# Selective scan laid out as 16 states by 8 channels on the partitions, with q and k projected during the scan

## What is computed

```python
qkv = einsum('bysd,ed->byse', x, w_qkv) + b_qkv          # 16 heads of 16
attn = softmax(einsum('bhqd,bhkd->bhqk', q, k) / sqrt(16))
vals = einsum('bhqk,bhkd->bhqd', attn, v)
h = concatenate([einsum('bse,oe->bso', vals, w_out) + b_out, txt], axis=1)   # 589 tokens
u = layernorm(h)
xp = einsum('bld,kd->blk', u, x_proj_w)                  # 64 + 16 (B) + 16 (C)
delta = softplus(einsum('blr,dr->bld', xp[..., :64], dt_proj_w) + dt_proj_b)
# for each token t, channel d (256) and state n (16):
#   h[d, n] = exp(delta[t, d] * A[d, n]) * h[d, n] + delta[t, d] * B[t, n] * u[t, d]
#   y[t, d] = sum over n of h[d, n] * C[t, n]
h = h + y + u * D_skip
```

## Time and profile before

| | us |
|---|---|
| median of 3 runs | 1422.09 |
| lowest, highest | 1415.88, 1423.06 |
| the profiled execution, its own time | 1426.25 |
| its span in the trace | 1424.1 |

### The profile page before, as it was taken

How to read it: one execution, slowest core, us unless ns; L and a number is a source line. 1 busy time by engine, 2 the same in 40 slices (tenths; PEclk the granted TensorE clock), 3 DMA queues, 4 the chain that set the end, 5 groups by cost and what they waited for, 6 DMA issues and landing times.

```text
span 1424.1 us, 14635 instructions
## 1 busy us (share of the span) xinstructions
PE 1044.0 (73%) x4633; PEld 522.9 (37%) x4634; DVE 790.0 (55%) x1271; ACT 457.2 (32%) x693; POOL 171.8 (12%) x217
## 2 busy tenths in 40 slices
PE   7898988888888988835653499995589955047780
PEld 2323332433234332422243255552366644023340
DVE  4603799768995799739935021223355558512224
ACT  1173356424663356442232111111122143011120
POOL 1000000000000000000002322211000002744451
PEclk9898989989998999967865599998699987568886
DMA  2197113111220113112255111112600000048856
GB/s 86 41 309 243 70 63 119 38 45 41 103 102 1 70 43 120 43 70 104 100 217 233 62 44 38 40 38 81 272 1 0 0 1 10 25 170 319 314 184 218
DMA packets 70254, 145.30 MB, mean 102 GB/s; under 512 B 10716, under 2 KB 54973, under 8 KB 66365
## 3 DMA queue, kind: packets, MB, share of 16 engines
q1 hardware_dynamic: 62720, 136.99, 27.9%
q0 software_dynamic: 7488, 7.70, 1.6%
HBM read 113.70 MB, written 43.75 MB: 111 GB/s over the span
## 4 chain that ended last, share of the span: by engine, by line
PE 33%; DVE 27%; issue 22%; POOL 6%; DMA 6%; ACT 5%; SPq 1%; POOLq 1%; DVEq 0%; ACTq 0%
DVE hst L1363 10%; PE ps L566 5%; DVE hC L1371 5%; PE ps L544 4%; DMA ys_dram<-yo,dest 3%; PE ps L863 3%; DVE mxn L1310 2%; PE ps L953 2%; PE ps L908 2%; PE ps L654 2%; POOL xs_dram L1285 2%; PE ps L676 2%; PE ps L881 1%; PE ps L667 1%; POOL ys_dram L1264 1%
## 5 line engine op out<-in xcount | busy, mean ns | idle before, releaser
L676 PE MATMUL ps<-hC,ident 128*128 128x512 f32 (+1 forms) x384 | 155.0, 544 | 72.7 <-DVE hC L1371 72.7
L1310 DVE TENSOR_REDUCE mxn<-ps 128x2 f32<-128x1024 f32 x128 | 151.3, 1221 | 74.2 <-PE ps L566 73.5
L1363 DVE TENSOR_TENSOR_SCAN hst<-dA,dBu 128x1180 f32<-128x1180 f32 x64 | 166.9, 2608 | 0.5
L1042 ACT ACTIVATE Ph<-ps 128x1024 f32<-128x1024 f32 x128 | 124.1, 1021 | 91.1 <-PE ps L654 91.1
L676 PEld LDWEIGHTS ps<-hC,ident 128*128 128x128 f32 x384 | 71.9, 201 | 184.8 <-DVE hC L1371 116.6
L566 PE MATMUL ps<-Kh,Qh 32*128 32x512 f32 x512 | 110.5, 694 | 16.1 <-DVE mxn L1310 13.8
L953 PE MATMUL ps<-ring,xgT 128*64 128x256 f32 x512 | 80.1, 440 | 27.0 <-DVE yo L1731 26.9
L654 PE MATMUL ps<-Qh,Kh 32*128 32x512 f32 x512 | 90.1, 684 | 4.6 <-ACT Ph L1042 4.6
L1354 DVE TENSOR_TENSOR dBu<-dtu,bc 128x1180 f32<-128x1180 f32 x64 | 87.9, 1378 | 0.0
L1249 POOL COPY xa<-home 128x20 f32<-128x20 f32 x1 | 0.2, 218 | 725.0 <-DMA home<-in_home 725.0
L1371 DVE TENSOR_TENSOR hC<-hst,bc 128x1180 f32<-128x1180 f32 x64 | 86.8, 1362 | 0.0
(11 more groups left out here) (239 smaller groups left out, 1477.2 us busy)
## 6 DMA issues: line engine op xcount, KB each, us to landing
bc<-bc_dram SPq DMA_DIRECT2D x64, 590.0 KB, 3.7
ring<-in_we SPq DMA_DIRECT2D x16, 2048.0 KB, 9.3
W<-in_w SPq DMA_DIRECT2D x14, 1024.0 KB, 18.3
xs_dram<-zeros SPq DMA_DIRECT2D x1, 8224.0 KB, 45.4
xg<-xs_dram SPq DMA_DIRECT2D x16, 514.0 KB, 4.3
yg<-ys_dram SPq DMA_DIRECT2D x12, 640.0 KB, 7.9
ys_dram<-zeros SPq DMA_DIRECT2D x1, 5120.0 KB, 49.6
xs_dram<-zeros SPq DMA_DIRECT2D x1, 4112.0 KB, 18.9
```

Source lines behind the costliest of these rows:

```text
L676: m = nc.tensor.matmul(tail[:, lo:hi], ident[:, :], state[:, lo:hi], start=False, stop=(n == NS - 1), skip_group_check=True)
L1042: nc.scalar.activation(Ph[:, n % 2, 2 * g:2 * g + 2, :], ps[:, 2 * g:2 * g + 2, :], ACT.Exp, scale=float(HD) ** -0.5).then_inc(act_p, 1)
L1310: nc.vector.tensor_reduce(slots32(mxn[:, hg % 2, i, :])[:, 2 * g:2 * g + 2, HD], ps[:, 2 * g:2 * g + 2, :], AX.X, ALU.max, negate=True).th ...
L1363: nc.vector.tensor_tensor_scan(hst[:, k % 2, :, :].rearrange("p c t -> p (c t)"), dA[:, k % 2, :, :].rearrange("p c t -> p (c t)"), dBu[:, ...
```

## The change

**Layout of the scan.** A unit now holds 8 channels with all 16 states on the 128 partitions (partition = 8·state + channel), again two such groups beside each other, so there are again 16 units (`UNITS`) for a sample. B and C are the same for all units of a sample and are spread once (`BC`, two loads). delta and delta·u, which were in SBUF for all units, differ for each unit: they are written to DRAM (`dd_dram`, two stores) and each unit loads them back with two loads of 590 KB, each of 8 rows repeated for 16 states (`spread`), into three slots `dd`. The operands of `decay` and `drive` come from `dd`. `output_gate` works in place on `hst`, which has four buffers, and `hC` is gone.

**Sum over the states.** Two units make a set of 32 channels. `add_set` adds it to y with eight matmuls: two pieces of tokens by four column tiles of 32, with 0/1 matrices `bsum`. One half of the channels is accumulated at a time, so `skip` and `take_y` are split in two.

**Projections.** q and k of sample b + 1 are projected while sample b is in `back` (on even steps, through bank 7), into a second buffer of `Qh` and `Kh`. Only v is projected in `front`, ahead of the first scores. Sample 0 still projects in its own front, through banks 5 and 6. `project_x` and `project_dt` come two groups of scores earlier. `Ph` and `OT` share their place with `xn`, `xb`, `sp` and `xpo`, so ACT starts the exponentials of a back only after `dd_out` and the first `decay`.

```diff
+            def spread(b, j):
+                k = UNITS * b + j
+                c, band, lane = place(j)
                 if k >= SLOTS:
                     q.wait_ge(dve_dBu, k - SLOTS + 1)
-                    q.wait_ge(dve_hC, k - SLOTS + 1)
-                q.dma_start(bc[:, k % SLOTS, :, :].rearrange("p w t -> p (w t)"),
-                            bc_dram[b, 2 * n:2 * n + 2].rearrange("(o w) t -> o (w t)", o=1).to_broadcast([P, 2 * LP])).then_inc(bc_in[k % SLOTS], 16)
+                    q.wait_ge(act_dA, k - SLOTS + 1)
+                for m in range(2):
+                    lo = HR * (lane + m) + DD * band
+                    q.dma_start(dd[:, k % SLOTS, m, :, :].rearrange("p w t -> p (w t)"),
+                                dd_dram[b, c, lo:lo + DD].rearrange("(o d) w t -> o d (w t)", o=1).to_broadcast([NS, DD, 2 * LP])).then_inc(dd_in[k % SLOTS], 16)
...
+                for w in range(2):
+                    q.dma_start(BC[:, w, :], bc_dram[b, w].rearrange("n (o t) -> n o t", o=1).to_broadcast([NS, DD, LP])).then_inc(bc_in, 16)
+                q.wait_ge(dve_delta, b + 1)
+                q.dma_start(dd_dram[b, :, :, 0, :].rearrange("c p t -> p c t"), sp[:, :, :]).then_inc(dd_out, 16)
+                q.wait_ge(dve_dtu, b + 1)
+                q.dma_start(dd_dram[b, :, :, 1, :].rearrange("c p t -> p c t"), xb[:, :, :]).then_inc(dd_out, 16)
+                q.wait_ge(dd_out, 32 * (b + 1))
+                for j in range(UNITS):
+                    spread(b, j)
...
+            def add_set(b, k):
+                c, band, _ = place(2 * k)
+                pe.wait_ge(dve_hC, UNITS * b + 2 * k + 2)
+                for lo, hi in pieces(0, LP):
+                    for lane in range(4):
+                        m = nc.tensor.matmul(tail[HR * lane:HR * (lane + 1), lo:hi], bsum[:, band, :], hst[:, (2 * k + lane // 2) % 4, lane % 2, lo:hi],
+                                             start=False, stop=(band == 3), skip_group_check=True)
                 m.then_inc(pe_y, 1)
...
+            def back(eb, cb, qb):
+                for n in range(NU):
                     if eb is not None:
                         tscores(eb, n)
+                        if qb is not None and n % 2 == 0:
+                            project(qb, n // 4, n // 2 % 2, 7)
                         if n:
                             weighted(eb, n - 1)
-                    if cb is not None and n >= 2:
-                        add_state(cb, n - 2)
+                    if cb is not None and n % 2 and n >= 3:
+                        if n == SETS + 3:
+                            skip(cb, 1)
+                        add_set(cb, (n - 3) // 2)
                 if eb is not None:
                     weighted(eb, NU - 1)
                     turn_heads(eb, range(HG - 1))
+                    turn_heads(eb, [HG - 1])
                 if cb is not None:
-                    add_state(cb, NS - 2)
+                    add_set(cb, SETS - 1)
...
+                softplus(nb)
+                act.wait_ge(dd_out, 32 * (nb + 1))
+                decay(nb, 0)
...
+            def drive(b, j):
+                k = UNITS * b + j
+                if j == 0:
+                    dve.wait_ge(bc_in, 32 * (b + 1))
+                dve.wait_ge(dd_in[k % SLOTS], 32 * (k // SLOTS + 1))
+                if k >= 2:
+                    dve.wait_ge(dve_scan, k - 1)
+                nc.vector.tensor_tensor(dBu[:, k % 2, :, :], dd[:, k % SLOTS, :, 1, :], BC[:, 0:1, :].to_broadcast([P, 2, LP]),
```

More of the change, by code:

```diff
@@ L622, in front @@
                     m.then_inc(pe_bo, 1)
+                else:
+                    project_v(mb, 0, 4)
+                    project_v(mb, 1, 3)
                 for hg in range(HG):
@@ L975, in _ @@
             front(0, None)
-            back(0, None)
+            back(0, None, 1)
             for b in range(NB):
-                nxt = b + 1 if b + 1 < NB else None
+                nxt, then = (k if k < NB else None for k in (b + 1, b + 2))
                 front(nxt, b)
-                back(nxt, b)
+                back(nxt, b, then)
             one_expert()
@@ L1073, in front @@
[L1073 to L1084 removed]
+                    take_v(mb, 0, 4)
+                    take_v(mb, 1, 3)
+                standard_deviations(nb)
@@ L1085, in back @@
+                normalise(nb)
+                take_u(nb)
+                take_x(nb)
+                softplus(nb)
+                act.wait_ge(dd_out, 32 * (nb + 1))
+                decay(nb, 0)
+            def back(eb, cb, qb):
+                for n in range(NU):
                     if eb is not None:
                         exps(eb, n)
+                        if qb is not None and n % 2 == 0:
+                            take_q(qb, n // 4, n // 2 % 2, 7)
                         if n % QT == 0 and n:
@@ L1088, in back @@
                             take_o(eb, n // QT - 1)
-                    if cb is not None and n + 1 < NS:
+                    if cb is not None and n == SETS + 2:
+                        take_y(cb, 0)
+                    if cb is not None and n + 1 < UNITS:
                         decay(cb, n + 1)
```

312 lines of the change are left out of this document (143 added, 169 removed).

## The result

The changed kernel is slower: 1464.32 us, median of 4 runs (1450.34 to 1468.55), beside 1418.99 us (1412.38 to 1423.06) of the kernel before on the same chip. The ratio is 1.031, 95% interval [1.022, 1.039]. I had predicted 1437, with 1415 to 1454: the direction was right, the loss is three times as large. Experiments named with one time and no range ran once each (e2, e5 to e10, e13, e14); the kernel before spread over 1404.6 to 1431.1 us in all its runs, so single runs are read here by the stages of their traces.

The account below looks back on a forecast made before the run. DVE was taken to bound scanning backs, PE and ACT alternating back(0, None), waits for scores the fronts. Terms +15 - 1.5 - 0.9 - 2 x (1.5 + 2.0) + 9.3 + 0 gave +14.9 on 1422.09: 1437 us, range 1415 to 1454.

Parts of the forecast that it names:

- Part 1, the scan units: Scans: still 64 units of 5.10 us with DVE never idle, 0 change, up to 60 if the loads bind.
- four loads of the present form move at 295 to 415 GB/s; these cover it: Scan units: the doubled loads need 237 GB/s, and the rate read from the kernel before was taken to suffice.
- loads bind: Rival in the scans: below 237 GB/s loads bind; at 200 GB/s a unit takes 6.0 us, +58, 1495; chance 0.05.
- DVE's small change of work in a unit: Scan units: the same three DVE operations of the same width, 5.10 us for each unit.
- PE's fall: Scanning backs: PE's busy time falls from 69 us to about 59 of 82 us.
- the `pe_y` wait: Scans: the new wait of `recurrence` on `pe_y` looks four units back, with almost one period of slack.
- The trip through DRAM: From the end of `dtu` to the first scan: store and loads take 14 us, mostly hidden except in sample 3.
- Part 2: back(0, None): projecting q and k there adds 15 us, bounds 8 and 16; a pair of groups grows to about 7.2.
- Part 3, the fronts: Three fronts, first scores to first scan: -6.0 at full clock, +4.5 for half clock, so -1.5 each.
- the clock term: Fronts: PE at half clock for about five of twelve groups ahead of `dtu`; 4.5 us taken, from 0 to 8.
- Parts 4 and 6: Joints: -0.9 ahead of front(1, 0), -2 twice; small things: 0, an extra constant +0.5 against shorter last sums -0.5.
- Part 5: Sample 3: joint gains 2, unhidden way from `dtu` to first scan costs +11.3; together +9.3, from 5 to 13.

Follow-up runs that it names:

- e2: Changed kernel with the repeat in the `dd` loads turned round, eight channels outermost and each row written to 16 partitions in a row: 1686.2 us.
- e5: Changed kernel with one source row for all partitions in the `dd` loads, written as 16 times 8 repeats (two outer dimensions): 1465.6 us.
- e10: Kernel before with its `bc` loads written as 16 times 8 repeats of the same row in place of 128: 1424.7 us, beside 1421.3.
- e13: Changed kernel with `dd` loads from 128 different rows, eight taken and eight left out 16 times (two outer dimensions): 1464.2 us.
- e14: Changed kernel with 16 loads for each unit, each of one row for one lane, repeated for 16 partitions eight apart: 1778.1 us.
- e6: Changed kernel with each `dd` load taken from 128 different rows, none repeated, one outer dimension: 1434.6 us.
- e1: Changed kernel with each `dd` load taken from one row repeated for all 128 partitions, in place of eight rows repeated 16 times: 1439.3 us.
- e15: Changed kernel with one-row `dd` loads (one outer dimension) and q and k of sample 1 projected in front(1, 0): 1428.1 us, ratio to before 1.009.

## Why the prediction was wrong

**Part 1, the scan units: the step that failed first.** I predicted 0 and it was +13.8 us in the scans. The step was "four loads of the present form move at 295 to 415 GB/s; these cover it". The changed loads are not of that form. They have a second outer dimension, and move 229 GB/s where a unit needs 237. The rival "loads bind" named the right threshold, and I gave it 0.05, arguing from rows of the same length. e5, e6 and e13, all with rows of that length, show that the form decided. The price was smaller than the rival's 58 us, since the rate is 3% below the need and not 16%: 1.21 MB at 229 GB/s are 5.28 us, 0.18 too long, and 64 times that is 11.5. DVE's small change of work in a unit, PE's fall and the `pe_y` wait were right: with fast loads all scans are 76.8 to 76.9 us (e1, e15).

**The trip through DRAM: right in its form, and slow by the same cause.** I predicted 14 us from the end of `dtu` to the first scan. With the loads of the form that I had priced it is 13.7 to 13.9 (e1); with the real ones it is 19.1, 17.5, 17.6 and 17.4. That is 16.4 us in all, and with the 13.8 of the scans 30.2; the span of e1 is 27.2 us shorter, its median time 25.0. So the loads account for about the whole distance from 1437 to 1464; that my other errors nearly cancel each other is luck.

**Part 2: right.** +13.8 for +15. A pair of groups went from 5.28 to 84.46 - 77.33 = 7.13 us (I had 7.2):

```profile
77.33 1.37 PE L690 MATMUL ps<-Qh,Kh 32*128 32x512 f32 x8
...
84.46 1.14 PE L690 MATMUL ps<-Qh,Kh 32*128 32x512 f32 x8
```

**Part 3, the fronts: the clock term was too small.** From the prediction's terms, 46.2 less 1.2 for the first scores, I had 45.0 us from first maximum to the end of `dtu` at full clock, and 4.5 for the half clock, so 49.5. Measured were 51.2, 53.6 and 53.2, and 51.1 to 53.9 in all the other fronts with this code, at mean clocks of 0.65 to 0.74. That is 6 to 9 for the clock in place of 4.5, if 45.0 is right, which nothing showed: no front without projections ran at full clock. With fast loads the three fronts cost 67.2, 66.0 and 67.2 us from first maximum to first scan, against 65.1, 65.0 and 65.0 before: +5.3 where I had -4.5. Of the fronts' miss (+17.0 for -4.5) 9.8 is the clock and 11.7 the loads. The pace was as predicted, 3.40 us for a group at half clock, but I had it for five of twelve groups, and mean clocks of 0.67 to 0.73 in these stretches mean half clock for more than half of the time:

```profile
515.50 2.36 DVE L1338 TENSOR_REDUCE mxn<-ps 128x2 f32<-128x1024 f32 x2 [1.24 <-PE ps L598]
518.90 2.36 DVE L1338 TENSOR_REDUCE mxn<-ps 128x2 f32<-128x1024 f32 x2 [1.04 <-PE ps L598]
522.31 2.36 DVE L1338 TENSOR_REDUCE mxn<-ps 128x2 f32<-128x1024 f32 x2 [1.05 <-PE ps L598]
```

**Parts 4 and 6: right in kind.** The joints gained 3.3 us each, near my 3.1 at full clock; I had taken 1.1 off for a half clock that did not come (1.00 in the joint). The extra constant cost nothing.

**Part 5:** +11.7 for +9.3: the trip took 3.4 us more than I had, the joint gained 1 more.

**What nobody predicted** are two stages that I had put at 0: front(0, None), +5.6, where the projections only use other banks, and the late part, -10.7, whose code is the same. From first to last maximum front(0, None) took 50.7 (e2) to 58.8 us (e15) with one and the same code, at mean clocks of 0.93 and 0.77; in the changed kernel 58.7, before 53.1. In these two spans they partly cancel, and a sum against one execution carries such errors whatever its terms.

## What to carry to other kernels

A price taken from a DMA holds for its access pattern, not for its size: before a load is moved near the bound, look whether the new source or destination has another outer dimension, and price it by a run. Work that fills gaps of PE in a stage where its clock falls to half may be free there, and taking it away may gain nothing; price such a move at both clocks. When a move doubles what a resource must carry, to 237 GB/s against 295 as the lowest rate read, and the form of access is new, the rival that it binds deserves more than 0.05.
